# Scores moved ahead of the values' projection, and the output projection moved into a half of another PSUM bank

## What is computed

```
x = x + 0.5 * ffn_stack(layernorm(x))
x = x + attn(layernorm(x))
x = x + 0.5 * ffn_stack(layernorm(x))

def ffn_stack(x):
    for i in range(6):
        x = attn_layer(shift_tokens(x), Wqkv[i], q_scale[i], k_scale[i], Wo[i]) + x
        x = ffn_layer(shift_tokens(x), ln_g[i], ln_b[i], W1[i], b1[i], W2[i], b2[i]) + x

def attn_layer(x, Wqkv, qs, ksc, Wo):          # 16 heads of 64, windows of 32 tokens
    q, k, v = split(x @ Wqkv)
    q, k = rotary(l2norm(q) * qs), rotary(l2norm(k) * ksc)
    attn = softmax(where(mask, -inf, q @ k_own_and_previous_window.T * 8))
    return (attn @ v_own_and_previous_window) @ Wo

def ffn_layer(x, g, b, W1, b1, W2, b2):        # 341 hidden values
    a, gate = split((layernorm(x) * g + b) @ W1 + b1)
    return (a * gelu(gate)) @ W2 + b2
```

## Time and profile before

| | us |
|---|---|
| median of 3 runs | 3282.68 |
| lowest and highest | 3281.99, 3286.73 |
| the profiled execution | 3285.78 |
| its span, first to last instruction | 3284.0 |
| TensorE's matmuls busy | 3149.2 (96%) |
| VectorE busy | 2675.4 (81%) |
| GpSimd busy | 2593.5 (79%) |
| ScalarE busy | 2355.0 (72%) |

### The profile page before, as it was taken

How to read it: one execution, slowest core, us unless ns; L and a number is a source line. 1 busy time by engine, 2 the same in 40 slices (tenths; PEclk the granted TensorE clock), 3 DMA queues, 4 the chain that set the end, 5 groups by cost and what they waited for, 6 DMA issues and landing times.

```text
span 3284.0 us, 149930 instructions
## 1 busy us (share of the span) xinstructions
PE 3149.2 (96%) x63424; PEld 2623.0 (80%) x63424; DVE 2675.4 (81%) x4403; ACT 2355.0 (72%) x4536; POOL 2593.5 (79%) x2894
## 2 busy tenths in 40 slices
PE   5999999999999999999779999999999999999997
PEld 4888888888888888888668888888888888888885
DVE  3888888888888888888558888888888888888884
ACT  3777777777777777777537777777777777777774
POOL 5987887888788878887349888878887888788772
PEclk7999999999999999999879999999999999999998
DMA  2221222222222222221112222222212222221211
GB/s 82 78 59 53 70 60 56 65 66 53 65 68 53 63 67 56 65 67 48 33 27 77 58 56 68 63 53 69 65 50 68 65 54 68 62 59 49 55 50 37
DMA packets 117857, 195.41 MB, mean 60 GB/s; under 512 B 23756, under 2 KB 36552, under 8 KB 117192
## 3 DMA queue, kind: packets, MB, share of 16 engines
q1 hardware_dynamic: 117192, 185.82, 21.2%
HBM read 33.71 MB, written 1.05 MB: 11 GB/s over the span
## 4 chain that ended last, share of the span: by engine, by line
PE 67%; DVE 17%; POOL 7%; issue 5%; ACT 2%; DVEq 0%; POOLq 0%; DMA 0%; ACTq 0%; SPq 0%
PE s_ps L925 8%; PE tr L969 7%; PE o_ps L954 7%; PE tr L938 5%; DVE ss_floor L721 4%; PE f_ps L1015 4%; PE qk_ps L866 4%; PE tr L866 4%; PE qk_ps L867 3%; PE qk_ps L868 3%; PE tr L893 3%; PE tr L906 3%; DVE rotated L714 3%; DVE rotated L708 2%; POOL rotated L420 2%
## 5 line engine op out<-in xcount | busy, mean ns | idle before, releaser
L420 POOL TENSOR_TENSOR rotated<-rotated 128x1024 f32<-128x1024 f32 x384 | 915.3, 2383 | 23.3 <-DVE rotated L714 23.3
L449 POOL TENSOR_TENSOR rotated<-rotated,rn 128x1024 f32<-128x1024 f32 x384 | 730.6, 1903 | 30.1
L426 POOL TENSOR_TENSOR prob<-prob,rden 128x512 f32<-128x512 f32 x384 | 436.5, 1137 | 326.7 <-DVE rden L746 325.7
L528 ACT ACTIVATE sq<-qk_ps 128x1024 f32<-128x1024 f32 x384 | 393.3, 1024 | 281.1 <-PE qk_ps L868 192.9
L708 DVE TENSOR_TENSOR rotated<-qk_ps,rot 128x1024 f32<-128x1024 f32 x384 | 469.3, 1222 | 140.4 <-ACT sq L528 126.4
L714 DVE TENSOR_TENSOR rotated<-qk_ps,rot 128x512 f32<-128x512 f32 x768 | 490.7, 680 | 0.0
L925 PEld LDWEIGHTS s_ps<-kt,qt 64*32 64x32 f32 x24576 | 361.4, 107 | 142.4 <-issue 126.3
L721 DVE TENSOR_REDUCE ss_floor<-sq 128x16 f32<-128x1024 f32 x384 | 464.1, 1209 | 0.4
L574 ACT ACTIVATE pt<-tr 128x512 f32<-128x512 f32 x384 | 229.3, 597 | 321.7 <-PE tr L938 320.3
L925 PE MATMUL s_ps<-kt,qt 64*32 64x64 f32 x24576 | 424.9, 218 | 1.7 <-issue 1.2
L969 PE MATMUL tr<-ot,wo 128*128 128x128 f32 x3072 | 406.7, 275 | 0.0
(11 more groups left out here) (152 smaller groups left out, 6949.9 us busy)
## 6 DMA issues: line engine op xcount, KB each, us to landing
vs<-vn SPq DMA_DIRECT2D x384, 192.0 KB, 2.5
vs<-vtail SPq DMA_DIRECT2D x384, 64.0 KB, 2.0
vtail<-vn SPq DMA_DIRECT2D x384, 64.0 KB, 2.2
staging<-layer_wqkv_dram SPq DMA_DIRECT2D x72, 256.0 KB, 3.0
wo<-layer_wo_dram SPq DMA_DIRECT2D x12, 512.0 KB, 3.9
xs<-xa SPq DMA_DIRECT2D x48, 128.0 KB, 2.3
fs<-xa SPq DMA_DIRECT2D x48, 128.0 KB, 2.3
xs<-xa SPq DMA_DIRECT2D x48, 127.8 KB, 2.4
```

Of the source, the lines that this page charges most:

```text
L420: nc.gpsimd.tensor_tensor(rot_c[h], rot_c[h], rot_s[h], ALU.add).then_inc(rot_added, 1)
L426: nc.gpsimd.tensor_tensor(prob[h][:, :, :], prob[h][:, :, :], rden[h][:, :].unsqueeze(2).to_broadcast([P, 2 * PAIRS, KEYS]), ALU.mult).the ...
L449: nc.gpsimd.tensor_tensor(folded, folded, rn[:, :].unsqueeze(2).to_broadcast([P, 2 * UH, DH]), ALU.mult).then_inc(qkn_ready, 1)
```

## The change

Three things are changed, all in TensorE's part and in one instruction of VectorE.

- `scores(n)` now stands directly behind `weigh_values(n - 2)`, and `project_v(n)` behind the scores.
- `project_out` writes columns 256 to 383 of the first bank of `o_ps`, which the weighed values leave free, and VectorE's add reads it from there.
- The waits follow. The queries' transposes wait for the last values' copy (`vn_ready`) and no more for the add. The weighing waits for the add of the unit before (`y_added`), since that add reads from a bank which the weighing writes. The output projection waits only for the add before it. The second gated product waits for the values' copy of its own slot in place of the add.

```diff
-                nc.vector.tensor_tensor(cols, tr0[:, 0:P], cols, ALU.add).then_inc(y_added, 1)
+                nc.vector.tensor_tensor(cols, o_ps[:, 0, HS:HS + P], cols, ALU.add).then_inc(y_added, 1)
...
             def query_heads(p, U):
                 h = U % 2
                 pe.wait_ge(qkn_ready, ONE + U + 1)
-                if live(p, U - 3):
-                    pe.wait_ge(y_added, ONE + U - 2)
-                else:
-                    pe.wait_ge(vn_ready, ONE + U)
+                pe.wait_ge(vn_ready, ONE + U)
...
-            def weigh_values(U):
+            def weigh_values(p, U):
                 TG, h = U // 2, U % 2
+                if live(p, U - 1):
+                    pe.wait_ge(y_added, ONE + U)
                 pe.wait_ge(pt_ready, ONE + U + 1)
...
             def project_out(p, U):
                 h, g = U % 2, U // UPL
                 pe.wait_ge(ot_ready, ONE + U + 1)
-                if live(p, U + 2):
-                    pe.wait_ge(vn_ready, ONE + U + 3)
-                else:
-                    pe.wait_ge(y_added, ONE + U)
+                pe.wait_ge(y_added, ONE + U)
                 if U % UPL == 0:
                     pe.wait_ge(wo_in, 16 * (g + 1))
                 for a in range(PAIRS):
-                    last = nc.tensor.matmul(tr0[:, 0:P], wo[g % 2][:, h, a, :], ot[h][:, :, a, :],
+                    last = nc.tensor.matmul(o_ps[:, 0, HS:HS + P], wo[g % 2][:, h, a, :], ot[h][:, :, a, :],
                                             start=a == 0, stop=a == PAIRS - 1)
...
                     if i == 1:
-                        pe.wait_ge(y_added, ONE + min(n - 1, (p + 1) * UPP))
+                        pe.wait_ge(vn_ready, ONE + min(n + 1, (p + 1) * UPP))
...
                     if live(p, n - 2):
-                        weigh_values(n - 2)
+                        weigh_values(p, n - 2)
                     if live(p, n):
+                        scores(n)
                         project_v(n)
-                        scores(n)
```

## The result

| | us |
|---|---|
| before, median of 4 runs | 3282.34 |
| after, median of 4 runs | 3376.18 (3374.83 to 3380.08) |
| ratio | 1.0287, 95% interval 1.0269 to 1.0305 |
| predicted | 3322, range 3290 to 3345 |

The changed kernel is 94 us slower, where 39 were forecast. The sign and the forecast waits came as predicted; the size did not, since one term was mis-sized and one was missing. The time lies 31 us above the range.

The account below looks back on a forecast made before the run. TensorE, busy 96% of the span, was taken as the bound, so its waits cost their full length. Terms summed to +39.3 us on the profiled 3285.8, giving 3325, or 3322 as median (1.2% slower); range 3290 to 3345.

Parts of the forecast that it names:

- The scores' wait for the keys: TensorE's scores, now without cover, wait for ScalarE's keys' copy plus a 0.06 us release: 0.22 to 0.34 us in most slots.
- kind 4: Slots with n mod 8 = 4, forecast like those with 5 and 7: wait 0.22, gain 0.14, net +0.08 us each.
- rival 3: Much slower: ScalarE becomes the loop, its late values' copy and those behind it delaying the next squares; 3380 us, chance 0.08.
- The switch of shapes: TensorE from scores to output projection: one change of array shape less, 2.27 us instead of 2.41, gain 0.14 a slot.
- Kind 1: Slots with n mod 8 = 1, behind the gates: scores wait 0.75 us for ScalarE's mask, gain 0.08, net +0.67.
- The gated products: FFN's second product no longer waits for VectorE's add; the fourth becomes late; gain 0.69 us in 31 slots.
- Kind 0: Slots with n mod 8 = 0, holding the FFN's gated products: 31 gain 0.69, 13 lose 0.15; together -18.6 us.
- Kind 3: Slots with n mod 8 = 3: scores wait 0.30 us as VectorE's lag shrinks by 0.20; net +0.16 a slot.
- GpSimd's waits: Transposes of probabilities waited 24 us for GpSimd's scaled probabilities; reaching that point later was taken as a 10 us gain.
- Rival 1: Faster: only the saved drain between array shapes counts, keys' copy landing before the weighing ends; 3206 us, chance 0.07.
- Rival 2: Hardly slower: earlier scores remove VectorE's and GpSimd's lag, saving 17 and 14 us; 3291 us, chance 0.12.
- kinds 0, 2 and 6: Slots with n mod 8 = 0, 2, 6: squares wait for VectorE's ss_floor, scores wait 0.34 us, net +0.20.

Follow-up runs that it names:

- e6_keys_wait_first: The changed kernel with the scores' two waits exchanged, the keys' copy written first and the mask second: 3354.6 us, 22 less than the changed kernel.
- e3_centre_first: The changed kernel with ScalarE's two centred copies of the FFN ahead of its values' copy: 3351.7 us, 24.5 less than the changed kernel.
- e13_both_misses: The changed kernel with both the centred copies ahead of the values' copy and the keys' wait written first: 3338.4 us against 3280.9 before, ratio 1.0178.
- e8_all_reorders: The changed kernel with ScalarE's queries' and keys' copies ahead of squares, centred copies ahead of values, mask ahead of exponentials behind the gates: 3298.1 us, ratio 1.0041.
- one half: The changed kernel with only the output projection's move to o_ps, the values' projection still ahead of the scores: 3257.8 us against 3279.1, ratio 0.9933.
- the other: The kernel before with only the scores put ahead of the values' projection, output projection still in tr0: 3530.6 us against 3279.1, ratio 1.0762.
- e9_reorders_values_first: The kernel with ScalarE's three new orders, as in e8_all_reorders, but the values' projection ahead of the scores: 3277.0 us, ratio 0.9985 to the kernel before.

## Why the prediction was right or wrong

1. **The scores' wait for the keys, right in mechanism, its term mis-sized.** 336 waits of TensorE on the keys' copy, some 340 forecast. The failed step is "That is the only kind of row for it; I take 0.06 with ends 0.02 and 0.12". The row was one of a single wait; the scores have two, and where the last to arrive is the second one written, 0.14 to 0.15 pass. It lay outside the bounds. Worth 22 us by `e6_keys_wait_first`, 20 in the slots alone.
2. **The missing term of kind 4.** The prediction followed the values' copy, 1.3 us later, to its own users and found cover for each ("its users come two slots later"), and in rival 3 it listed what stands behind that copy in kind 7, but asked only whether the next squares would be late. It did not go through what is queued behind the copy in kind 4, whose user, the variances' matmuls, stands in the same slot. 24.5 us by `e3_centre_first`: 26 in kind 4, of which 6 come back in kind 5, and the rest outside the slots. The rule was in the prediction's own words, "behind the waiting scores stand ... all the rest of TensorE's queue"; it was not applied to ScalarE.
3. **The switch of shapes, right:** 2.27 us from scores to output projection, measured 2.27. The unknown step from packed to packed was put at 0 to 0.1, hidden; it is as dear as the one it replaces, and hidden.
4. **Kind 1, right:** 44 waits on the mask, 0.68 us each at the matmul and 0.79 at the weight load; forecast 0.75 (+0.62 a slot, measured +0.50).
5. **The gated products, right:** the second without idle, the fourth the next to be late by 0.17 where 0.14 was worked out. Kind 0 as a whole gained 0.19 and not 0.39, 10 us less: the 31 slots that had waited for the add gained 0.47 each and not 0.69, and the other 13 lost 0.35 and not 0.15. The release of step 1 is 0.09 in both; with both misses out (`e13_both_misses`) it is 0.59 and 0.26.
6. **Kind 3, right in sign:** VectorE's lag shrank, net +0.21 against +0.16.
7. **GpSimd's waits, right in sign:** the transposes' waits for GpSimd at the weight loads, the 24.1 us of the earlier trace rows, fell to 7.8 us in 15. That is 16 less where I took 10; the same waits seen at the matmuls fell from 11.1 to 3.8.
8. **The rivals.** Rival 1 fell: every plain slot idles before the scores. Rival 2 fell in its larger part: the squares of kinds 0, 2 and 6 still start 0.15 behind the end of qk, and their scores wait 0.11 longer than those of 4, 5 and 7; VectorE's add waits for the output projection 310 times. Its other part, GpSimd's waits, came for the most part (step 7). Rival 3's time of 3380 lies next to the measured one, but its mechanism did not happen: in slot 120 the squares start at 1043.65, 0.15 behind the end of qk as in kinds 0, 2 and 6 before. The right number there would have been for a wrong reason; what of it was true is that ScalarE's copies behind the values' one came too late for somebody, and that was TensorE's variances and not the squares.

Sum: 39 forecast, 22 and 25 for the two misses, would give 86 of 94. But out together the two are worth 38, and `e13_both_misses` is still 57 us above the kernel before. Its slots are 54 us longer, some 14 over the forecast: 5 of them in kind 0, 7 in kind 5 (mostly the idle inside the scores' run), and 2 where kinds 4 and 6, which held GpSimd's waits, gave back 8 and not 10.

## What to carry to other kernels

When a step is moved behind another on the engine that sets the time, look at what covered its inputs: here the values' projection covered the keys' copy by 0.89 us, and no saved step between array shapes (0.14 us) could pay for it. When one instruction becomes late on a second engine, list everything that stands behind it in that engine's queue, slot kind by slot kind, with each user's place, and not only its own users. Try a change of two edits in halves: one half was worth -0.7%, the other +7.6%, and together +2.9%, so they don't add and the sum hid both. And look inside a run of small matmuls too: with the wait ahead of the scores gone, `e8_all_reorders` idled for 50 us in the middle of their run, where no semaphore shows.

## What the runs showed of the hardware

A TensorE step with two semaphore waits starts about 0.06 us behind the releasing copy's end when the wait written first is the last to be met, and 0.14 to 0.15 when it is the one written second, which the trace shows as an instruction of its own of 0.05 us ahead of the weight load. Exchanging them moved 22 us of 3376. I had not expected the order of two waits to matter.

The step from 64x64 tiles to 64x32 tiles takes as long as the step from 64x64 tiles to the full array: 0.23 us from the start of the last group of eight matmuls to the next start in both, where the groups themselves follow at 0.12.

A run of 64 small matmuls directly behind another one can idle in its middle with no semaphore to wait for: some 50 us at 70 places in `e8_all_reorders`, each 1.24 to 1.71 us after the end of a 16 KB transfer of instructions. With the three large matmuls of the values' projection between the two runs (`e9_reorders_values_first`) it was 3 us.
